# Second-norm statistics on ScalarE, gates and expert matrices batch by batch, and one masked product in an AdaLN block

## The reference

```python
mod = (silu(c) @ wmod).reshape(8, 6, 1, 128)          # sa, ca, ga, sb, cb, gb; |ga|, |gb| at least 0.25
h = layernorm(x) * (1 + ca) + sa
x = x + ga * attn(h)
h = layernorm(x) * (1 + cb) + sb
x = x + gb * (h + sum_e gates[b, e] * (h @ A[e].T) @ Bw[e].T)   # 8 experts of rank 64
# attn, per head (8 heads of 16):
q, v = relu(h @ enc_q), relu(h @ enc_v)
dist[t, j] = sqrt(sum(metric * (q[t] - q[t - j])**2) + 1e-8)     # j = 0..63, causal
w = exp(-dist) of the 32 nearest, else 0
context = (w / (w.sum() + 1e-8)) @ v + gate * 0.1 * (q / |q|) @ hebb
out = (q * context) @ decoder
```

## Time and profile before

| | |
|---|---|
| runs | 685.01, 686.34, 686.57 us; median 686.34 |
| profiled execution | 686.94 us, span 685.2 us |
| PE busy | 615.5 us, 90% of the span |
| DVE busy | 602.9 us, 88% |
| ACT busy | 519.2 us, 76% |
| POOL busy | 488.4 us, 71% |

### The profile page before, as it was taken

How to read it: one execution, slowest core, us unless ns; L and a number is a source line. 1 busy time by engine, 2 the same in 40 slices (tenths; PEclk the granted TensorE clock), 3 DMA queues, 4 the chain that set the end, 5 groups by cost and what they waited for, 6 DMA issues and landing times. The chain is left out here.

```text
span 685.2 us, 22680 instructions
## 1 busy us (share of the span) xinstructions
PE 615.5 (90%) x6050; PEld 432.1 (63%) x6114; DVE 602.9 (88%) x4954; ACT 519.2 (76%) x1574; POOL 488.4 (71%) x717
## 2 busy tenths in 40 slices
PE   4997887899999999999999999999999999999876
PEld 2543444566776676666666666666666666667654
DVE  4895458899999999999999999999999999999860
ACT  2896125688888888888888888888888888888752
POOL 3111314788888888888888888888888888888662
PEclk9998566899999999999999999999999999999999
DMA  7220000000001010001010101010001000000000
GB/s 212 77 77 5 10 9 20 16 22 27 23 27 28 26 28 27 27 27 28 27 27 26 28 26 28 26 28 26 27 27 28 26 24 28 27 26 25 18 12 16
DMA packets 41183, 21.22 MB, mean 31 GB/s; under 512 B 6040, under 2 KB 40544, under 8 KB 41056
## 3 DMA queue, kind: packets, MB, share of 16 engines
q1 hardware_dynamic: 41056, 19.77, 10.1%
HBM read 10.44 MB, written 4.19 MB: 21 GB/s over the span
## 5 line engine op out<-in xcount | busy, mean ns | idle before, releaser
L1009 DVE MAX8 top<-modn_all 128x8 f32<-128x32 f32 x2048 | 207.1, 175 | 6.4
L562 POOL TENSOR_TENSOR big<-big,con 128x512 f32<-128x512 f32 x128 | 160.4, 1275 | 22.4 <-DVE big L1068 22.4
L1015 DVE MATCH_REPLACE8 modn_all<-top,modn_all 128x32 f32<-128x32 f32 x1024 | 166.4, 173 | 0.0
L1260 PE MATMUL psC<-vst,big 128*128 128x68 f32 x512 | 103.0, 283 | 9.7 <-POOL big L562 7.7
L502 POOL TENSOR_TENSOR wmod_sb<-key,meet 128x512 f32<-128x512 f32 x64 | 67.8, 1060 | 51.8 <-DVE meet L1096 51.8
L1261 PE MATMUL psC<-vst,big 128*128 128x68 f32 x512 | 99.7, 276 | 0.0
L1260 PEld LDWEIGHTS psC<-vst,big 128*128 128x128 f32 x512 | 78.3, 193 | 31.4 <-POOL big L562 30.6
L1261 PEld LDWEIGHTS psC<-vst,big 128*128 128x128 f32 x512 | 78.7, 194 | 0.0
L1015 DVE MATCH_VALUE_LOAD modn_all<-top,modn_all 128x8 f32 x1024 | 77.3, 75 | 0.0
L771 ACT ACTIVATE psD<-key 128x256 f32<-128x256 f32 x64 | 24.8, 388 | 51.0 <-issue 47.7
L1286 PE MATMUL psW<-sqs,selm 128*16 128x192 f32 x256 | 55.9, 343 | 2.8 <-POOL sqs L512 2.8
(11 more groups left out here) (215 smaller groups left out, 1578.4 us busy)
## 6 DMA issues: line engine op xcount, KB each, us to landing
tst<-qT_all SPq DMA_DIRECT2D x256, 17.0 KB
big<-in_x SPq DMA_DIRECT2D x16, 256.0 KB, 2.8
xs<-in_x SPq DMA_DIRECT2D x64, 64.0 KB, 1.9
out<-yo SPq DMA_DIRECT2D x64, 64.0 KB, 1.6
sst<-nst SPq DMA_DIRECT2D x128, 3.0 KB
tst<-nst SPq DMA_DIRECT2D x128, 2.0 KB
con<-in_consts SPq DMA_DIRECT2D x1, 581.5 KB, 6.8
wmod_sb<-in_wmod SPq DMA_DIRECT2D x1, 384.0 KB, 5.8
```

The lines of the kernel that those rows point to most:

```text
L562: nc.gpsimd.tensor_tensor(wab[:, k % 2, v].rearrange("p (r t) -> p r t", r=4), wsel.rearrange("p (r t) -> p r t", r=4), part.unsqueeze(1). ...
L1009: last = v.max(top[:, u, h, where], low_high[:, u, h])
L1015: last = v.match_replace(low_high[:, u, h], top[:, u, h, 1:9], low_high[:, u, h], GONE)
L1260: mm(o, wab[:, k % 2, 0, cols], vst[:, blk + 1:blk + 3, r], start=True, stop=False)
```

## The change

- **Statistics of the second norm.** DVE's two instructions go. ACT sums the rows of `x2` while it copies them (an accumulated output), makes the negative mean, squares the deviations with another accumulated sum, and takes logarithm and exponential, one after the other, directly behind the copy. Its three instructions at the start of a step go.
- **Denominator.** The 1e-8 is added by a matmul of one row into the context's PSUM columns; DVE only takes the reciprocal.
- **One masked product.** DVE writes the unmasked weights into `wab`; POOL makes the product with `of_own` alone and a difference of neighbouring value blocks (`vdif`). PE multiplies the unmasked weights by the earlier blocks and the masked ones by the difference.
- **Gates and matrices batch by batch.** `gate_weights`, `expert_matrices`, both halves of `bsc` and the sixteen wide matmuls go. With the distances of chunk 0 of a batch PE issues the two gate rows, with those of chunk 3 the expert sum of that batch, both into free columns of the distances' banks; DVE takes them up ahead of line 1052's work, and POOL makes `bsc` for one batch in every eighth step.
- **Order at the start.** Parts of the routing move: on PE behind other work of steps -3 and -2, on DVE into steps -1 and 0. The first chunk's copy to PSUM no longer waits for the second chunk's distances, which wait for the first `pairs` instead.

The core of the diff (removed: also `gate_weights`, POOL's `routing`):

```diff
+    c[0, C_TINY] = 1e-8
...
+        pGate = [psD[:, r].rearrange("p (g x) -> p g x", g=NG)[:, :, PW + HW:PW + HW + D // 2] for r in range(3)]
+        pDen = pC.rearrange("p (n x) -> p n x", x=VD)[:, :, HD]
...
+        def gates_with(k):
+            return k // CPB if k % CPB == 0 else None
+        def expert_with(k):
+            return k // CPB if k % CPB == 3 else None
...
+                if there(i) and i % CPB == 0:
+                    b = i // CPB
+                    pool.wait_ge(r0_dve, 10)
+                    need(pool, gb_ready, b)
+                    nc.gpsimd.tensor_tensor(bsc[:], b_sb[:], gate_er[:, :, b:b + 1].broadcast_to([P, 4, D]),
+                                            ALU.mult).then_inc(bsc_ready, 1)
...
+                    blk = 2 * (k % CPB)
+                    pool.wait_ge(vst_ready, 2 * k + 2)
+                    need(pool, c_ready, k - 1)
+                    nc.gpsimd.tensor_tensor(vdif[:, k % 2], vst[:, blk + 1:blk + 3], vst[:, blk:blk + 2],
+                                            ALU.subtract).then_inc(vdif_ready, 1)
                     pool.wait_ge(w_ready, k + 1)
-                    need(pool, c_ready, k - 1)
-                    for v, part in enumerate((of_own, of_before)):
-                        nc.gpsimd.tensor_tensor(wab[:, k % 2, v].rearrange("p (r t) -> p r t", r=4),
-                                                wsel.rearrange("p (r t) -> p r t", r=4),
-                                                part.unsqueeze(1).broadcast_to([P, 4, CH]), ALU.mult).then_inc(wab_ready, 1)
...
-                k = i - 4
-                if there(k):
-                    s = k % 2
-                    act.wait_ge(mvc_ready, k + 1)
-                    need(act, nc_ready, k - 1)
-                    need(act, rs_done, k)
-                    nc.scalar.activation(lv_c[:], mv_c[:, s, 1:2], ACT.Ln, bias=bias[:, 0:1]).then_inc(lnc_done, 1)
-                    nc.scalar.activation(nm_c[:, s:s + 1], mv_c[:, s, 0:1], ACT.Copy, scale=-1.0).then_inc(nm_done, 1)
-                    act.wait_ge(lnc_done, k + 1)
-                    nc.scalar.activation(rs_c[:, s:s + 1], lv_c[:], ACT.Exp, scale=-0.5).then_inc(rs_done, 1)
...
+                    s = k % 2
                     act.wait_ge(att_ready, k + 1)
                     need(act, y_ready, k - 1)
-                    nc.scalar.activation(x2[:, k % 2], pAtt, ACT.Copy).then_inc(x2_ready, 1)
+                    need(act, rs_done, k)
+                    nc.scalar.activation(x2[:, s], pAtt, ACT.Copy, accum_out=sum_c[:]).then_inc(x2_ready, 1)
+                    act.wait_ge(x2_ready, k + 1)
+                    nc.scalar.activation(nm_c[:, s:s + 1], sum_c[:], ACT.Copy, scale=-1.0 / D).then_inc(nm_done, 1)
+                    act.wait_ge(nm_done, k + 1)
+                    nc.scalar.activation(dev_c[:], x2[:, s], ACT.Square, bias=nm_c[:, s:s + 1],
+                                         accum_out=ssq_c[:]).then_inc(ssq_done, 1)
+                    act.wait_ge(ssq_done, k + 1)
+                    nc.scalar.activation(lv_c[:], ssq_c[:], ACT.Ln, bias=bias[:, 0:1], scale=1.0 / D).then_inc(lnc_done, 1)
+                    act.wait_ge(lnc_done, k + 1)
+                    nc.scalar.activation(rs_c[:, s:s + 1], lv_c[:], ACT.Exp, scale=-0.5).then_inc(rs_done, 1)
...
-                    act.wait_ge(dist_ready, min(k + 2, NCH))
+                    if k:
+                        act.wait_ge(dist_ready, min(k + 2, NCH))
...
-                    dve.wait_ge(r0_dve, 10)
-                    for kt in range(2):
-                        v.tensor_tensor(bsc[:, kt], b_sb[:, kt].unsqueeze(1).broadcast_to([P, NB, D]),
-                                        gate_er[:, kt].unsqueeze(2).broadcast_to([P, NB, D]), ALU.mult).then_inc(bsc_ready, 1)
-                if i == 1:
-                    expert_matrices(0)
-            def expert_matrices(half):
-                four = slice(4 * half, 4 * half + 4)
-                dve.wait_ge(pG_ready, half + 1)
-                need(dve, gb_ready, half)
-                link(v.tensor_tensor(mI[:], (psC, psX)[half][:].rearrange("p (b d) -> p b d", b=4),
-                                     ident.unsqueeze(1).broadcast_to([P, 4, D]), ALU.add))
-                v.tensor_tensor(g_b[:, four], g_b[:, four], mI[:], ALU.mult).then_inc(gb_ready, 1)
+            def gates(b):
+                halves = "p (g x) -> p g x"
+                v.tensor_tensor(dec_b[:, b].rearrange(halves, g=NG), dec_sb[:].rearrange(halves, g=NG), pGate[0],
+                                ALU.mult).then_inc(gatew_ready, 1)
+                v.tensor_copy(g_b[:, b].rearrange(halves, g=NG), pGate[1]).then_inc(gatew_ready, 1)
+            def expert(b):
+                g = g_b[:, b].rearrange("p (g x) -> p g x", g=NG)
+                dve.wait_ge(gatew_ready, 2 * b + 2)
+                v.tensor_tensor(g, g, pGate[2], ALU.mult).then_inc(gb_ready, 1)
...
-                    need(dve, rden_ready, k - 1)
-                    v.tensor_scalar(den[:, s], cst[:, s, :, HD], 1e-8, None, ALU.add).then_inc(den_done, 1)
...
+                    if gates_with(k) is not None:
+                        gates(gates_with(k))
+                    if expert_with(k) is not None:
+                        expert(expert_with(k))
                     e = key[:, k % 2].rearrange("p (h j) -> p h j", h=NH)
                     v.scalar_tensor_tensor(out=e, in0=pB, scalar=0.0, in1=e, op0=ALU.max, op1=ALU.min).then_inc(d2_ready, 1)
+                    if k == 0:
+                        dve.wait_ge(r0_pe, 5)
+                        v.tensor_copy(gateT[:], psX[0:NE, 152:152 + NB]).then_inc(r0_dve, 1)
...
-                    v.reciprocal(rden[:, k % 2], den[:, k % 2]).then_inc(rden_ready, 1)
+                    dve.wait_ge(cst_ready, 2 * k + 2)
...
-                    v.bn_stats(st_c[:], x2[:, k % 2]).then_inc(stc_ready, 1)
...
-                    v.bn_aggr(mv_c[:, k % 2], st_c[:]).then_inc(mvc_ready, 1)
...
-                    pe.wait_ge(bsc_ready, 4)
-                    pe.wait_ge(gatew_ready, NB // 2)
-                    for half, bank in enumerate((psC, psX)):
-                        for kt in range(4):
-                            last = mm(bank[:], a_sb[:, kt], bsc[:, kt, 4 * half:4 * half + 4].rearrange("p b d -> p (b d)"),
-                                      start=(kt == 0), stop=(kt == 3))
-                        last.then_inc(pG_ready, 1)
...
+            def gate_rows(b):
+                for u in range(2):
+                    last = mm(pGate[u], con[0:NB, b:b + 1].broadcast_to([NB, P]), gn[:, u].rearrange("b (g x) -> b g x", g=NG),
+                              start=False, stop=True, skip_group_check=True)
+                return last
+            def expert_sum(b):
+                pe.wait_ge(bsc_ready, b + 1)
+                for kt in range(4):
+                    mm(pGate[2], a_sb[:, kt], bsc[:, kt].rearrange("p (g x) -> p g x", g=NG), start=False, stop=False,
+                       skip_group_check=True)
+                return mm(pGate[2], ident, ident.rearrange("p (g x) -> p g x", g=NG), start=False, stop=True,
+                          skip_group_check=True)
...
-                    pe.wait_ge(wab_ready, 2 * k + 2)
-                    for r in range(4):
-                        cols = slice(r * P, (r + 1) * P)
-                        o = pC[:, r * 2 * VP:(r + 1) * 2 * VP].rearrange("p (v x) -> p v x", v=2)
-                        mm(o, wab[:, k % 2, 0, cols], vst[:, blk + 1:blk + 3, r], start=True, stop=False)
-                        last = mm(o, wab[:, k % 2, 1, cols], vst[:, blk:blk + 2, r], start=False, stop=True)
+                    def context(part, values, first):
+                        for r in range(4):
+                            o = pC[:, r * 2 * VP:(r + 1) * 2 * VP].rearrange("p (v x) -> p v x", v=2)
+                            done = mm(o, wab[:, k % 2, part, r * P:(r + 1) * P], values[:, :, r], start=first and r == 0,
+                                      stop=not first, skip_group_check=True)
+                        return done
+                    pe.wait_ge(w_ready, k + 1)
+                    context(0, vst[:, blk:blk + 2], True)
+                    pe.wait_ge(vdif_ready, k + 1)
+                    pe.wait_ge(wab_ready, k + 1)
+                    last = context(1, vdif[:, k % 2], False)
+                    last = mm(pDen, con[0:1, C_ID:C_ID + 1].broadcast_to([1, P]),
+                              con[0:1, C_TINY:C_TINY + 1].broadcast_to([1, 4 * NG * 2]), start=False, stop=True,
+                              skip_group_check=True)
...
+                    if k == 1:
+                        pe.wait_ge(pair_done, 2)
                     for r in range(NR):
                         masks(r)
-                    distances(k % 2).then_inc(dist_ready, 1)
+                    last = distances(k % 2)
+                    if gates_with(k) is not None:
+                        last = gate_rows(gates_with(k))
```

(44 more changed lines are left out.)

106 lines of the change are left out of this document (29 added, 77 removed).

## The result

The changed kernel takes **705.0 us** (median of 4 runs, 703.4 to 707.7), the kernel before 686.2 beside it: ratio 1.028, 95% interval 1.024 to 1.032. It is slower by 18.8 us; 702.9 was forecast (+16.6), with 682 to 718 as the range. The profiled execution is the longest of the four, 707.7 us for a span of 705.8; spans differ by 705.8 − 685.2 = 20.6.

A forecast was written before the change was run, and what follows sets the result against it. The prediction took a ring through ACT, DVE and POOL, 8.63 us a turn, to bound the kernel. Statistics +19.9, batches +5.3, head −7 and tail −1.6 summed to +16.6: 702.9 us, range 682 to 718.

The forecast's parts named there:

- The ring: Loop: ACT's `key` through its line 787 copy, DVE's scan, POOL's subtraction, back to `key`; 8.63 us, said to set steps.
- a turn: One pass from ACT's line 707 to the next, through DVE and POOL: 8.63 us before, 9.06 forecast with the change.
- the middle of the bounds: ACT's squares in the statistics chain: 0.36 us assumed, between copies of 0.27 and 0.46 us.
- DVE's and POOL's savings worth nothing: Loop: DVE's 0.70 us a step at most, and POOL's second product, count for nothing, since both engines already wait.
- The denominator's matmul at nothing: PE in the loop, ahead of the difference's transposes: extra matmul costed at nothing; otherwise 0.23 us a step, 14 us.
- the cover: PE's wait for POOL's subtraction before transposing the difference, said to hide the denominator's extra matmul.
- The batches: Gate and expert matmuls on PE delay line 778 in two of eight steps: 0.75 us a batch, +5.3 us in all.
- The head: Before the third scan: DVE products and idling go, the first expert sum comes; −7 us, bounds −3 and −12.
- The tail: Last steps, `x2` copy to POOL's normalisation: 3.32 us becomes some 1.7, −1.6 us.
- The chain did not fit: Rival: line 771 starts within 1.12 us of the `x2` copy, turn stays 8.63 us; 683 us, chance 0.13.
- DVE does not set the step: Rival claimed DVE sets the step, so its 0.70 us comes off each: 635 us, chance 0.04.
- The clock held in the loop: Rival claimed PE loses its clock in the loop, some 3 us a batch, 21 us on top: 724 us, chance 0.08.

The follow-up runs named there:

- the copy ahead: Changed kernel with ACT's copy of the picked values to PSUM issued ahead of the logarithm and the root: 692.0 us, ratio 1.010.

## Why the prediction was right, and where it was off

**The ring and the statistics: right, to a few hundredths.** Forecast 1.55 us from the `x2` copy to the copy to `psD`, 1.88 to the logarithm, a turn of 9.06 and +19.9 us; measured 1.59, 1.89, 9.06, and 19.8 us for this part by itself. (The chain was 0.04 longer than forecast and the hop to the logarithm 0.03 shorter, so the last hundredth is luck.) The squares take 0.40 us; the middle of the bounds was 0.36. By the Trainium skill (ScalarE: Activation LUTs, section "What ACT_TABLE_LOAD costs") they would take 386 ns: nearer than the middle, and the trace agrees to within 0.02 us. The readouts stand as in the earlier trace rows: issued 0.09 to 0.12 us before the activation's end here, 0.19 to 0.20 long.

**DVE's and POOL's savings worth nothing: right.** DVE's busy time between 200 and 600 us fell from 386.9 to 354.1, and the scan's wait grew from 0.37 to 0.69 us.

**The denominator's matmul at nothing: right for a regular step, for the reason given.** Undoing it leaves that at 9.06, and without the cover it costs. Behind an expert or a gate step PE is late and the cover is used up: there the matmul costs 0.12 us, 2.0 us over the loop. The price named for the case without cover was too low: 0.31 to 0.32 us a step, not 0.23.

**The batches: the mechanism right, the size short.** The step that failed is "0.03 + 0.72 = 0.75 us a batch". The expert sum is as forecast: the transposes' end was put at 2.60 us after the copy, and the logarithm starts at 2.62; its interval is 0.74 longer than a regular one. The gates are not: their four passes take 448.76 − 448.12 = 0.64 us where 0.46 was priced, so they delay the logarithm by 2.08 − 1.89 = 0.19, not 0.03. And the step behind each of the two is 0.12 us longer, for which the prediction had no term; it is the denominator's matmul that lengthens it, as the run without that shows. In all 1.0 to 1.25 us a batch instead of 0.75, 2 to 3.5 us over the loop.

**The head: the number right, in part by luck.** It is 7.7 us against 7, but not by the terms added up. The first scan comes 105.13 − 100.48 = 4.65 us earlier; the other 3.0 us lie between it and the third, where the kernel before runs at 0.50 and the changed one at 1.00 (the windows from 115 to 120); whether the clock is all of it was not separated. The first expert sum, priced at half clock with 2.3 us, took 109.47 − 108.25 = 1.22. And the size varies: in the four other profiled runs with this head and without the copy ahead the third scan comes between 117.0 and 120.2.

**The tail: the wait shrank as said, and the clock took the gain in this profile.** Forecast was −1.6 us; from the sixty-first scan to the end the kernel is 0.8 longer, where 3 × 0.33 − 1.6 = −0.6 was forecast. The rows of ACT, PE and POOL there:
```profile
693.66 0.27 ACT L764 ACTIVATE x<-psX 128x128 f32<-128x128 f32 x1
...
697.56 0.27 ACT L811 ACTIVATE oT<-psX 128x128 f32<-128x128 f32 x1
```
```profile
694.12 0.77 PE L1344 MATMUL psX<-x,con 128*128 128x128 f32 x2 [1.01 <-ACT h2T L756]
...
695.24 1.65 PE L1218 MATMUL psX<-mask_bf,ident_bf 128*1 128x256 bf16 x7
...
697.93 0.30 PE L1301 MATMUL psX<-con,n_c 128*128 128x128 f32 x1
```
```profile
695.51 0.45 POOL L534 TENSOR_SCALAR n_c<-x,nm_c,rs_c 128x128 f32<-128x128 f32 x1 [0.65 <-ACT rs_c L773]
```
From the copy to POOL's normalisation it is 695.51 − 693.66 = 1.85 us instead of 3.32. But `n_c` is ready at 695.96 and PE takes it up at 697.93 only, behind seven fillers, a transpose and ACT's copy of that (`oT`, line 811), at a granted clock of 0.57 (the window from 694 to 698 above). The run with the statistics alone has the same pieces at 1.00 (694 to 698):
```profile
695.24 0.46 PE L1329 MATMUL psX<-x,con 128*128 128x128 f32 x2 [1.06 <-ACT x L754]
...
695.85 0.93 PE L1227 MATMUL psX<-mask_bf,ident_bf 128*1 128x256 bf16 x7
...
697.67 0.30 PE L1297 MATMUL psX<-con,n_c 128*128 128x128 f32 x1 [0.27 <-ACT oT L800]
```
From line 1329 (here 1344) to the transpose of `n_c` it takes 2.43 us there, 3.81 here, and 677.26 − 673.85 = 3.41 in the kernel before. So 1.0 of the 1.6 us is gained, since PE then waits for `oT` instead, and the low clock costs 1.4. That run's part from the sixty-first scan on is 705.4 − 655.15 = 50.25 us against 51.1 before, 0.8 shorter where 0.6 was forecast.

**The rivals.** The chain did not fit: 1.59 us is past 1.12. DVE does not set the step. The clock held in the loop, and what the prediction counted in its favour, that "the fillers stay", was the reason, as the run without them shows. The price of 3 us a fall in that rival stands in no row; without the fillers a step in which the clock fell is 1.2 to 2.3 us longer. The busy share that it gave, "about 91%", was wrong: 383 of 400 us, 96%, since PE got more to do.

**What lay outside the prediction.** The prediction looked at one ring and at what covers each edit. It did not ask how far the next bound is. PE at 8.75 us stood 0.31 us behind the changed ring, its additions hidden by nothing but the ring. That is why undoing the statistics gives back only half of what they cost.
